# Zeros of the key stacks sent along with the keys, each stacked row in 16 pieces of 1 KB

## What is computed

```python
x = x + xattn(layernorm(x), ctx_1024, ctx_1024, Wq, bq, Wk, bk, Wv, bv, Wo, bo)
x = x + ffn(layernorm(x), ...)
# xattn: q = Q @ Wq.T + bq, k = K @ Wk.T + bk, v = V @ Wv.T + bv, in 16 heads of 8
#        scores = q k^T / sqrt(8); attn = softmax(scores); ctx = attn v; ctx @ Wo.T + bo
# ffn:   two small gated bottlenecks give softmax scores; the 32 largest of 128 gate x and x @ weight
```

## Time and profile before

| what | us |
|---|---|
| median of 3 runs (lowest, highest) | 531.14 (529.52, 537.45) |
| the profiled execution | 530.78 |
| its span | 529.0 |
| attention stage: first to last key stack issued | 23.49 to 249.76 |

### The profile page before, as it was taken

How to read it: one execution, slowest core, us unless ns; L and a number is a source line. 1 busy time by engine, 2 the same in 40 slices (tenths; PEclk the granted TensorE clock), 3 DMA queues, 4 the chain that set the end, 5 groups by cost and what they waited for, 6 DMA issues and landing times.

```text
span 529.0 us, 16337 instructions
## 1 busy us (share of the span) xinstructions
PE 393.7 (74%) x5502; PEld 306.8 (58%) x5516; DVE 411.9 (78%) x1941; ACT 393.8 (74%) x1069; POOL 361.0 (68%) x514
## 2 busy tenths in 40 slices
PE   3455989999999999999897435766685685586543
PEld 1124677777877787777785224555574564465442
DVE  7555566767776877677764299999999999999946
ACT  3414667877887788786675568889999999999863
POOL 7356766788786777865211202569999999989996
PEclk9999988999999999999999556697769768878865
DMA  5787788778878887777500000000000000000011
GB/s 156 160 210 180 164 204 204 182 196 203 186 177 188 189 208 188 188 176 179 124 7 2 0 0 2 1 1 22 22 20 20 22 21 22 21 22 20 22 39 60
DMA packets 138970, 53.02 MB, mean 100 GB/s; under 512 B 105146, under 2 KB 131195, under 8 KB 137339
## 3 DMA queue, kind: packets, MB, share of 16 engines
q1 hardware_dynamic: 136712, 51.47, 40.3%
q10 hardware_dynamic: 2176, 0.52, 0.5%
HBM read 34.67 MB, written 16.78 MB: 97 GB/s over the span
## 4 chain that ended last, share of the span: by engine, by line
SPq 30%; DVE 27%; PE 11%; ACT 9%; DMA 9%; issue 6%; POOL 6%; DVEq 0%; POOLq 0%; ACTq 0%
SPq L295 27%; DVE tops L1050 11%; DVE kst L1062 11%; DMA k_scratch<-k_parts 6%; ACT kst L775 3%; SPq L280 2%; DMA qst<-q_scratch 2%; PE ps_pv L355 2%; POOL kst L1229 1%; ACT kst L786 1%; PE ps_row L530 1%; PE ps_col L340 1%; PE ps_col L530 1%; ACT kst L823 1%; PE ps_row L384 1%
## 5 line engine op out<-in xcount | busy, mean ns | idle before, releaser
L900 DVE TENSOR_REDUCE m<-ps_row 128x8 f32<-128x512 f32 x128 | 82.3, 685 | 53.1 <-PE ps_row L384 53.1
L646 ACT ACTIVATE pT<-ps_col 128x512 f32<-128x512 f32 x128 | 68.6, 588 | 30.3 <-PE ps_col L340 30.3
L1050 DVE MAX8 tops<-kst 128x8 f32<-128x128 f32 x384 | 78.5, 265 | 0.0
L355 PE MATMUL ps_pv<-vx,pT 128*64 128x18 f32 x2048 | 72.8, 213 | 0.0
L355 PEld LDWEIGHTS ps_pv<-vx,pT 128*64 128x64 f32 x2048 | 66.4, 139 | 6.9 <-ACT pT L646 3.5
L1062 DVE MATCH_REPLACE8 kst<-tops,kst 128x128 f32<-128x128 f32 x264 | 69.0, 266 | 0.0
L384 PE MATMUL ps_row<-kst,qst 96*64 96x128 bf16 x1024 | 41.6, 224 | 11.0 <-DMA qst<-q_scratch 11.0
L340 PEld LDWEIGHTS ps_col<-qst,kst 100*128 100x128 bf16 x1024 | 33.9, 99 | 23.9 <-issue 11.5
L340 PE MATMUL ps_col<-qst,kst 100*128 100x64 bf16 x1024 | 41.6, 195 | 7.1 <-DMA qst<-mT 7.1
L558 PE MATMUL ps_pv<-idb,kst 128*128 128x128 bf16 x120 | 10.9, 243 | 42.3 <-ACT kst L786 42.1
L384 PEld LDWEIGHTS ps_row<-kst,qst 96*64 96x64 bf16 x1024 | 32.5, 113 | 14.8 <-DMA qst<-q_scratch 13.1
(11 more groups left out here) (157 smaller groups left out, 1256.3 us busy)
## 6 DMA issues: line engine op xcount, KB each, us to landing
k_scratch<-k_parts SPq DMA_DIRECT2D x32, 192.0 KB, 3.0
q_scratch<-q_parts SPq DMA_DIRECT2D x32, 192.0 KB, 3.0
kst<-k_scratch SPq DMA_DIRECT2D x32, 192.0 KB
qst<-q_scratch SPq DMA_DIRECT2D x32, 192.0 KB
xr<-in_x_dram SPq DMA_DIRECT2D x16, 256.0 KB, 3.9
cT<-in_ctxT_dram SPq DMA_DIRECT2D x16, 256.0 KB, 3.6
kst<-k_scratch SPq DMA_DIRECT2D x32, 128.0 KB
qst<-q_scratch SPq DMA_DIRECT2D x32, 128.0 KB
```

Of the source, the lines that this page charges most:

```text
L355: mm = pe.matmul(pv_flat[pp * SEQ:(pp + 1) * SEQ, h * 2 * VW:(h + 1) * 2 * VW], pT[:, 2 * j + pp, hh, :], vx[s][:, 2 * hp + pp, h, :], sta ...
L646: act.activation(pT[:, b % PT_RING, :, :], ps_col[b % 2][:, :, :], ACT.Exp, scale=SCALE).then_inc(act_exp, 1)
L900: dve.tensor_reduce(m32[:, b // 4, :, 4 * j:4 * j + 4].rearrange("q a h -> q h a"), ps_row[b % 2][:, :, :, :], AX.X, ALU.max).then_inc(dve ...
L1050: ins = dve.max(top[:, n, :], src)
```

## The change

The scratch rows of the keys hold the zeros too: [a, part, feature, 512 keys and zeros, 32 unused] (`GAP`), 1088 B a row, of which 1 KB is written. A stacked row then is 16 heads x 1 KB; source pieces have 64 B between them, the destination row has none. `k_parts` becomes three views into one tile, `k_frames`, zeroed once by VectorE; the splits on POOL write runs of 64 keys with 64 columns between them. For a = 1 the frame is read from 64 columns earlier, so that zeros come first. The memsets of the three `kst` and the waits for them go; SP issues the three minus rows and then x of group 2 at once. `write_parts` becomes `write_keys` and `write_queries`, with the same waits; the query DMAs name the same bytes with one more dimension.

```diff
@@ -38,6 +38,8 @@
 CTX_RING = 4
 STACK = 16 * 2 * len(RUNS)
 WRITES = 16 * 2
+
+GAP = 32
 RESTS = 12
 
 
@@ -79,7 +81,9 @@
         q_rest = sb("q_rest", [128, GTOK])
         k_rest = sb("k_rest", [128, GTOK])
         q_parts = sb("q_parts", [128, PARTS, GTOK], BF16)
-        k_parts = sb("k_parts", [128, PARTS, GTOK], BF16)
+
+
+        k_frames = sb("k_frames", [128, 2 * (PARTS * GTOK + SEQ)], BF16)
         vx = [sb(f"vx{s}", [128, PAIRS, HEADS, 2 * VW]) for s in range(2)]
         pT = sb("pT", [128, PT_RING, HEADS // 2, SEQ])
         attn = sb("attn", [128, 2, 2, DIM])
@@ -133,7 +137,9 @@
         y_sb = [room[s][:, n:n + 512].rearrange("p (t c) -> p t c", t=PAIRS) for s, n in ((0, 3072), (1, 3072), (2, 0))]
         sides, sidesT = [room[s][:, 3584:4096].bitcast(BF16).rearrange("p (n c) -> p n c", n=2 * PAIRS) for s in range(2)]
         q_scratch = [nc.dram_tensor(f"q_scratch{s}", (2, PARTS, 128, HALF), BF16).ap() for s in range(2)]
-        k_scratch = [nc.dram_tensor(f"k_scratch{s}", (2, PARTS, 128, HALF), BF16).ap() for s in range(2)]
+        k_scratch = [nc.dram_tensor(f"k_scratch{s}", (2, PARTS, 128, GTOK + GAP), BF16).ap() for s in range(2)]
+        k_parts = [k_frames[:, :].rearrange("c (a x) -> c a x", a=2)[:, :, n * GTOK:(n + 1) * GTOK]
+                   .rearrange("c a (p m) -> c a p m", p=PAIRS)[:, :, :, 0:SEQ] for n in range(PARTS)]
         xsT = q32
         yin = [b[:, :].rearrange("q (p c) -> q p c", p=PAIRS) for b in (k32, k_rest)]
         tops = [sb(f"tops{s}", [128, 2 * PAIRS, TOPK]) for s in range(2)]
@@ -189,7 +195,6 @@
         dve_ab, dve_ve2, dve_nm2 = sem("dve_ab"), sem("dve_ve2"), sem("dve_nm2")
 
         gp_rs1, gp_rs2, gp_split, gp_xb, gp_bn = (sem(f"gp_{n}") for n in ("rs1", "rs2", "split", "xb", "bn"))
-        gp_zero = sem("gp_zero")
 
         p2_x2T, p2_lin, p2_full, p2_xsT, p2_yin = (sem(f"p2_{n}") for n in ("x2T", "lin", "full", "xsT", "yin"))
         p2_sidesT, p2_order, p2_aheadT = sem("p2_sidesT"), sem("p2_order"), sem("p2_aheadT")
@@ -256,43 +261,43 @@
                              (wf_sb, ffn_w), (lin_sb, lin_w), (bf_row, bf), (marks_sb, marks), (steps_sb, steps)):
                 sp.dma_start(dst[:, :], src).then_inc(rest_in, 16)
             sp.dma_start(gates[2 * GATES:2 * GATES + 1, :], ones_row).then_inc(rest_in, 16)
+
             for s in range(STACKS):
-
-                if s == 1:
-                    sp.wait_ge(gp_zero, 1)
-                else:
-                    sp.wait_ge(dve_zero, s // 2 + 1)
-                if s == 2:
-                    load_x(2)
                 sp.dma_start(kst[s][MROWS:KROWS, :, :, :, :].rearrange("r h p a m -> r (h p a m)"), minus_rows).then_inc(rows_in, 16)
-
-            def write_parts(g, parts, scratch, done, moved):
+            load_x(2)
+
+            def write_keys(g):
                 s = g % 2
-                if parts is k_parts:
-                    wait(sp, gp_split, 4 * g + 4)
-                else:
-                    wait(sp, dve_split, 4 * min(g + 1, 2))
-                    wait(sp, gp_qsplit, 4 * (g - 1))
+                wait(sp, gp_split, 4 * g + 4)
                 if g >= 2:
 
-                    wait(sp, moved[slot(g - 2)], STACK * uses(g - 2))
+                    wait(sp, k_moved[slot(g - 2)], STACK * uses(g - 2))
                 for a in range(2):
-                    sp.dma_start(scratch[s][a].rearrange("n c t -> c n t"),
-                                 parts[:, :, a * HALF:(a + 1) * HALF]).then_inc(done[s], 16)
-
-            def stack(g, scratch, done, moved, to_keys):
+                    sp.dma_start(k_scratch[s][a, :, :, 0:GTOK].rearrange("n c t -> c n t"),
+                                 k_frames[:, a * PARTS * GTOK:(a + 1) * PARTS * GTOK].rearrange("c (n t) -> c n t", n=PARTS)
+                                 ).then_inc(k_out[s], 16)
+
+            def write_queries(g):
+                s = g % 2
+                wait(sp, dve_split, 4 * min(g + 1, 2))
+                wait(sp, gp_qsplit, 4 * (g - 1))
+                if g >= 2:
+                    wait(sp, q_moved[slot(g - 2)], STACK * uses(g - 2))
+                for a in range(2):
+                    sp.dma_start(q_scratch[s][a].rearrange("n c t -> c n t"),
+                                 q_parts[:, :, a * HALF:(a + 1) * HALF]).then_inc(q_out[s], 16)
+
+            def stack(g, scratch, out, moved, stacks, first_part):
                 s, d = g % 2, slot(g)
-                wait(sp, done[s], WRITES * (g // 2 + 1))
+                wait(sp, out[s], WRITES * (g // 2 + 1))
                 for a in range(2):
                     for n in RUNS:
-                        first = PARTS - n if to_keys else 0
-                        src = scratch[s][a, first:first + n].rearrange("n (i h) t -> (n i) (h t)", h=HEADS)
-                        rows = spread(a, n)
-                        dst = (kst[d][rows, :, :, a, :].rearrange("r h p m -> r (h p) m") if to_keys
-                               else qst[d][rows, :, :].rearrange("r h t -> r (h t)"))
-                        if to_keys:
-                            src = src.rearrange("r (x m) -> r x m", m=SEQ)
-                        sp.dma_start(dst, src).then_inc(moved[d], 16)
+                        first = first_part(n)
+                        src = scratch[s][a, first:first + n].rearrange("n (i h) t -> (n i) h t", h=HEADS)
+                        sp.dma_start(stacks[d][spread(a, n)], src[:, :, 0:stacks[d].shape[2]]).then_inc(moved[d], 16)
+
+            kst_rows = [kst[s][:, :, :, :, :].rearrange("r h p a m -> r h (p a m)") for s in range(STACKS)]
+            qst_rows = [qst[s][:, :, :] for s in range(STACKS)]
 
             for t in range(FIRST, LAST + 1):
                 if 2 <= t + 3 < GROUPS:
@@ -303,11 +308,11 @@
 
                     wait(sp, act_mT, 2 * t)
                     wait(sp, pe_col, 8 * (t - 1))
-                    stack(t + 1, k_scratch, k_out, k_moved, True)
-                    stack(t + 1, q_scratch, q_out, q_moved, False)
+                    stack(t + 1, k_scratch, k_out, k_moved, kst_rows, lambda n: PARTS - n)
+                    stack(t + 1, q_scratch, q_out, q_moved, qst_rows, lambda n: 0)
                 if there(t + 2):
-                    write_parts(t + 2, k_parts, k_scratch, k_out, k_moved)
-                    write_parts(t + 2, q_parts, q_scratch, q_out, q_moved)
+                    write_keys(t + 2)
+                    write_queries(t + 2)
 
             for g in range(GROUPS):
                 if g < GROUPS - 1:
@@ -952,7 +957,7 @@
 
             dve.memset(half_neg[:, :], -0.5).then_inc(dve_half, 1)
             dve.memset(nothing[:, :], 0.0).then_inc(dve_half, 1)
-            dve.memset(kst[0][:, :, :, :, :].bitcast(F32).rearrange("r h p a m -> r (h p a m)"), 0.0).then_inc(dve_zero, 1)
+            dve.memset(k_frames[:, :].bitcast(F32), 0.0).then_inc(dve_zero, 1)
             for t in range(FIRST - 1, LAST + 2):
                 if there(t - 1):
                     row_max(t - 1, 6)
@@ -999,7 +1004,6 @@
                 if t < 0:
                     first_stats(t + 4)
                 if t == FIRST:
-                    dve.memset(kst[2][:, :, :, :, :].bitcast(F32).rearrange("r h p a m -> r (h p a m)"), 0.0).then_inc(dve_zero, 1)
                     for s in range(2):
                         dve.memset(vx[s][:, :, :, :].rearrange("k p h v -> k (p h v)"), 0.0).then_inc(dve_frame, 1)
                     dve.wait_ge(dve_frame, 2)
@@ -1121,14 +1125,17 @@
                 wait(pool, act_k, g + 1)
                 if g >= 1:
                     wait(pool, k_out[(g - 1) % 2], WRITES * ((g - 1) // 2 + 1))
+                else:
+                    pool.wait_ge(dve_zero, 1)
+                keys, rest = [b[:, :].rearrange("c (a p m) -> c a p m", a=2, p=PAIRS) for b in (k32, k_rest)]
                 wait(pool, gp_split, 4 * g)
-                pool.tensor_copy(k_parts[:, 2, :], k32[:, :]).then_inc(gp_split, 1)
+                pool.tensor_copy(k_parts[2], keys).then_inc(gp_split, 1)
                 wait(pool, gp_split, 4 * g + 1)
-                pool.tensor_tensor(k_rest[:, :], k32[:, :], k_parts[:, 2, :], ALU.subtract).then_inc(gp_split, 1)
+                pool.tensor_tensor(rest, keys, k_parts[2], ALU.subtract).then_inc(gp_split, 1)
                 wait(pool, gp_split, 4 * g + 2)
-                pool.tensor_copy(k_parts[:, 1, :], k_rest[:, :]).then_inc(gp_split, 1)
+                pool.tensor_copy(k_parts[1], rest).then_inc(gp_split, 1)
                 wait(pool, gp_split, 4 * g + 3)
-                pool.tensor_tensor(k_parts[:, 0, :], k_rest[:, :], k_parts[:, 1, :], ALU.subtract).then_inc(gp_split, 1)
+                pool.tensor_tensor(k_parts[0], rest, k_parts[1], ALU.subtract).then_inc(gp_split, 1)
 
             def split_queries(g):
                 wait(pool, act_q, g + 1)
@@ -1142,7 +1149,6 @@
                 wait(pool, gp_qsplit, 4 * (g - 2) + 3)
```

(1 more changed line is left out.)

## The result

The changed kernel takes 614.22 us (median of four runs, 609.03 to 619.66) against 533.89 us for the kernel before, run beside it: 1.148 times the time of before, 95% interval 1.133 to 1.163. All ratios here are taken over the fast runs alone, since some executions of either kernel are over 1.5% longer than its fastest. The forecast was 555 us with a range of 522 to 575. The direction was right, the size was not: +80 us instead of +24.

The account below looks back on a forecast made before the run. The bound was taken to be an end-to-end train of DMA transfers. 1.1 + 0.9 - 0.5 = +1.5 us a period, +22.5 over 15 periods, plus 1 for the last group: 530.8 + 23.5 = 554.3, said as 555 us, range 522 to 575.

Parts of the forecast that it names:

- rival C: SP's queue, not the engines, is the bound: key issue shrinks 2.2 us a period; about 508 us; chance 0.14.
- Step 2: Key write: packets go from 512 B to 1 KB, +0.9 us a period (bounds +0.7 and +1.3).
- Step 5: Splits on POOL, now in strided pieces of 64: 0, with +1 us a group hidden by POOL's slack.
- Step 6: Start of the kernel, with memsets removed and an earlier first key write: 0 (bounds -2 and +1 us).
- Step 1: Key stack: 64 pieces of 128 B become 16 of 1 KB at 61 ns, +1.1 us a period (bounds -0.7 and +2.9).
- the line: DMA packet price from 512 B and 2 KB packets: 8 ns plus 37 ns for each KB, 46 ns for 1 KB.
- Rival A: Stack DMAs: two engines always write into one place, 70 ns a piece on average; about 576 us; chance 0.17.
- Step 3: Query stack: same 8 KB rows, SP's pace no longer limiting, -0.5 us a period (bounds 0 and -1.5).
- Step 4: Query write, context and x loads, row maxima: unchanged, 0, filling the time between key write and next key piece.

Follow-up runs that it names:

- e_by8: The changed kernel with keys and queries in 8-row DMAs, 8 of 12 row sets eight partitions apart, the last four sets four apart; 671.66 us (1.263).
- b_even: The kernel before with 16-row stack DMAs only, last key part and first query part twice in the scratch; 534.56 us (1.011).
- e_qlate: The changed kernel with SP's wait for the first row maxima placed between key stack and query stack; 586.96 us (1.108).
- e_parts: The changed kernel with twelve key DMAs of 8 rows instead of six of 24, 16 and 8; 588.37 us (1.110).
- e_write: The kernel before with the frames and the 1 KB key write, key stacks still of 128 B pieces; 545.93 us (1.027).
- e_by4: The changed kernel with keys and queries in 8-row DMAs, rows four partitions apart; 631.55 us (1.187).
- e_even: The changed kernel with both sequences' rows in one DMA (48, 32 and 16 rows, two partitions apart); 610.87 us (1.147).
- e_mfirst: The changed kernel with SP holding key and query writes until the step's first row maxima are ready; 617.56 us (1.161).

## Why the prediction was wrong

**What held.** The bound before was read rightly: a train of transfers, with SP's long issues as its effect. SP's issue of the keys fell to 4.4 us and brought nothing, so rival C is wrong. Step 2, the key write, was +0.9 and measured +1.0 a period, with 45 ns a piece where 46 was taken. Step 5, the splits, held: 610 and 1158 ns, as before. Step 6, the start, is a small miss: 0 with -2 to +1 was given, and it is +1.4. The first key write is issued at 12.16 us, over 2 us earlier, but takes 12.2 us to land instead of 8.7.

**Step 1 was mis-sized.** A key piece was taken at 61 ns and takes 75. I had scaled by the query rows (430 ns against 307). Those rows are a poor measure of a full train, I now think, for in the kernel before SP issues them no faster than the engines move them, so that engines seldom meet; no run shows this. The better row stood there too: the 16 KB rows of neighbouring partitions at 1.7 us, nearly three times their line. It had served as the upper bound. That this bound, 76 ns, is nearly the 75 measured is luck: it left out the 8 ns that each piece has by the line (8 + 2 x 38 = 84), and 75 is a mean over pieces that share a place and pieces that don't. Where the engines share places two by two, a piece took 87 ns (e_by8). Rival A is thus right as to the mechanism, and the pair with steps of four and of eight shows it: 49 against 87 ns, with nothing changed but the partitions. A 128 B piece seems not to feel this. It costs 13 ns in the kernel before and in b_even, whose rows lie on other partitions (149 to 153 us: 0.953 x 64 us / 4704); at that price two engines ask for 20 GB/s where about 26 can go. That reason is an estimate, not a run.

**Step 3 stays open.** Its gain of 0.5 us for the queries was not measured alone. Its sum is also off: eight rows at 0.43 us are 3.4 us, not 3.7, and at 0.307 us 2.5, a bound of -1.7 and not -1.5. Neither would have changed the outcome.

**Step 4 was wrong in kind.** It reads "Query write, context and x loads, row maxima. Unchanged, 0." The row maxima's DMA was 16 KB and off the path, and so I gave it nothing. The runs show a loop there. SP starts keys and queries; 8 to 11 us later ScalarE issues the first row maxima (168.44, in the timeline above); they land only when what SP had issued ahead has moved; TensorE's scores of the group, the next projection and the second row maxima follow; then SP may start again. In the chain of the changed kernel for two later steps:

```profile
208.61 0.28 ACT mT L688
...
208.96 8.91 DMA qst<-mT
...
217.92 1.04 PE ps_col L345 x16
218.96 1.01 PE ps_mix L375 x4
219.97 1.71 PE ps_proj L409 x2
...
232.90 0.28 ACT mT L688
...
233.25 6.48 DMA qst<-mT
```

In the kernel before, I take it, full queues held SP back at the key stack, which kept what stood in front of the row maxima short. No run slows SP's hand-over alone: e_qlate, in which SP hands the queries over later, gains 27 us, and e_parts, in which it hands the keys over more slowly, gains 26, but has cheaper pieces too. In the changed kernel SP hands over keys and queries in 9 us, but the last query row starts only 14 to 16 us after the first key DMA was issued. The row maxima's DMA then takes 5.8 to 8.9 us. Step 1 said that SP's issue falls and "that is hidden by the engines' 7.4 us", and this passed the effect by: the shorter issue was no gain, and it seems to have done harm.

Part of the harm is the clock. In the long wait before 217.9 us TensorE is nearly idle from 212 us on and its granted clock is 0.50 from 214 us on, and it is still 0.50 in 224 to 226 us; L409's pair of matmuls takes 1.71 us after this wait. In the shorter wait before it (TensorE is idle in 196 to 198 us) the clock stayed at 1.00, and the same pair took 0.86 us.

**The sum.** A period grew by 4.8 us: 1.0 by the write (measured alone), 1.3 in the loop (19.9 against 18.6 with the queries held back, which fits the 1.5 us a period in which the changed kernel's DMA engines stand still, and is a lower bound, since that run still waits), and the rest, 2.5, is put down to the key pieces, between e_write's 16.1 and that run's 18.6. I had forecast +1.5, and missed 3.3: 1.9 in the piece's price and the queries' supposed gain (2.5 where steps 1 and 3 had 1.1 - 0.5), 1.3 in a wait for which the sum had no term, 0.1 in the write. The split rests on the two runs' difference, not on an experiment in which the pieces alone are cheap; none was tried that leaves 16 KB rows on partitions that reach all 16 places evenly. Rival A, which had the right mechanism for the pieces, gave 576 us; with no term for the loop it was too low as well.

## What to carry to other kernels

Larger descriptors pay only where the path behind them can take the rate that they ask for: count the rows of a DMA by the partitions that share a way in, and price the new piece by the slowest transfer of the trace into few partitions, not by the ones over all 128. And before a producer's issue is made cheaper, ask what its being held back kept short. A small DMA on another queue that the next step waits for can stand behind all that was handed over before it, as here; to put one wait between two large hand-overs gave back 27 of 80 us.

## What the runs showed of the hardware that was not expected

- Two engines that write rows 32 partitions apart share about 26 GB/s: 87 ns for a 1 KB piece instead of 49, with eight engines in both cases (e_by8, e_by4). All 16 engines writing rows that lie two thirds in partitions 0 to 63 reach 218 GB/s (e_even, 162 to 166 us).
- A 16 KB DMA issued on ScalarE's queue takes 8 us while 1.5 MB of keys and 0.8 MB of queries, issued before it on SP's queue, are under way, even when no later writes are in front (8.06 and 8.62 us in e_mfirst). Its first packet starts 4.1 to 5.7 us after the issue, against 1.2 to 2.7 in the kernel before. The other queue was no way around them here.
- Moving the start of every 1 KB piece to a multiple of 256 B changed the engines' busy time by 1% (4265 to 4215 us) and the kernel's time not at all (614.22 and 614.71 us).
